# One unrolled pipeline over single batches in place of two looped stages at the end of a six-stage kernel

## The reference, cut to what matters

```python
# fifth block: x are the latents, ctx_1024 the context
xn, ln_lat = layer_norm(ctx, g1, b1), layer_norm(latents, g2, b2)
q = ln_lat @ Wq
kv = jnp.concatenate([xn, ln_lat], axis=1) @ Wkv
weight = jnp.einsum('bhld,bhnd->bhln', q * scale, k * scale)
weight = softmax(jnp.where(full_mask, weight, neg))
out = einsum('bhln,bhnd->bhld', weight, v) ... @ Wout
# sixth block
h = bitlinear(x, norm1_w, w1)        # rmsnorm, rows rounded to 8 bits, weights to -1, 0, 1
h = act_scale * jnp.square(jax.nn.relu(h)) + act_bias
y = bitlinear(h, norm2_w, w2)
```

## Time and profile before

| | us |
|---|---|
| median of 3 runs (lowest, highest) | 2016.25 (2013.10, 2018.52) |
| profiled execution, device time | 2015.99 |
| its span in the trace | 2014.2 |
| latents phase, first context load to barrier | 1183.9 to 1825.7 |
| last phase (its weights rounded by 1834.2) | 1828.6 to 2014.2 |
| DVE busy in the last 17.0 us of the latents' setup | 1.53 |

### The profile page before, as it was taken

How to read it: one execution, slowest core, us unless ns; L and a number is a source line. 1 busy time by engine, 2 the same in 40 slices (tenths; PEclk the granted TensorE clock), 3 DMA queues, 4 the chain that set the end, 5 groups by cost and what they waited for, 6 DMA issues and landing times. The chain is left out here.

```text
span 2014.2 us, 28424 instructions
## 1 busy us (share of the span) xinstructions
PE 1525.4 (76%) x10850; PEld 793.9 (39%) x10850; DVE 1358.7 (67%) x2359; ACT 829.6 (41%) x1141; POOL 361.7 (18%) x309
## 2 busy tenths in 40 slices
PE   5788767777778768888888738999999999983222
PEld 3555444454433323333333424444444444431111
DVE  3765655767555579888888617575675675466997
ACT  2222122322234358888888723332332332313444
POOL 2232212323200021111110013332322322120000
PEclk9889868887778879999999959999999999996555
DMA  3000000000000000000000010000000000000000
GB/s 135 1 1 2 1 11 12 6 12 6 1 0 0 0 1 1 1 1 1 1 1 1 1 53 6 6 5 0 5 5 0 5 0 0 0 0 0 11 10 21
DMA packets 14814, 16.46 MB, mean 8 GB/s; under 512 B 640, under 2 KB 13056, under 8 KB 14336
## 3 DMA queue, kind: packets, MB, share of 16 engines
q1 hardware_dynamic: 14432, 14.47, 2.1%
q10 hardware_dynamic: 288, 0.67, 0.1%
HBM read 13.04 MB, written 2.10 MB: 8 GB/s over the span
## 5 line engine op out<-in xcount | busy, mean ns | idle before, releaser
L1427 POOL PARTITION_BROADCAST l_share<-l_recip x128 | 103.9, 812 | 376.5 <-issue 207.0
L1283 ACT ACTIVATE l_prob<-psum,l_bias_now 128x1024 f32<-128x1024 f32 x64 | 71.3, 1114 | 221.3 <-PE psum L1191 221.3
L1349 DVE TENSOR_REDUCE l_top<-psum 128x8 bf16<-128x1024 f32 x64 | 77.3, 1207 | 126.2 <-PE psum L1177 124.5
L1216 PE MATMUL psum<-l_prob,l_X 128*128 128x512 f32 x256 | 124.9, 611 | 12.7 <-DVE l_px L1343 12.7
L1185 PE MATMUL psum<-l_th,l_XT 128*128 128x512 f32 x256 | 126.0, 615 | 7.2 <-ACT l_prob L1283 7.2
L1343 DVE TENSOR_TENSOR l_px<-psum,l_share 128x1024 f32<-128x1024 f32 x64 | 78.0, 1219 | 71.7 <-PE psum L1216 45.3
L1161 PE MATMUL psum<-l_XT,l_A 128*128 128x512 f32 x256 | 117.5, 604 | 9.3 <-ACT l_XT L1269 9.3
L1240 PE MATMUL psum<-l_px,l_N 128*128 128x512 f32 x256 | 111.5, 593 | 2.1 <-DVE l_px L1343 2.1
L1337 DVE CAST l_th<-l_th 128x512 bf16<-128x512 f32 x128 | 89.3, 739 | 29.2 <-ACT l_th L1272 29.2
L1356 DVE RECIPROCAL l_recip<-psum 128x512 f32<-128x512 f32 x32 | 107.1, 3347 | 0.7 <-PE psum L1206 0.6
L1272 ACT COPY l_th<-psum 128x512 f32<-128x512 f32 x128 | 74.2, 586 | 74.5 <-PE psum L1161 74.5
(11 more groups left out here) (301 smaller groups left out, 3309.2 us busy)
## 6 DMA issues: line engine op xcount, KB each, us to landing
early_weights<-in_weights SPq DMA_DIRECT2D x1, 2405.0 KB, 15.1
c_cs<-in_ctx SPq DMA_DIRECT2D x8, 256.0 KB, 2.8
l_mats<-in_l_mats SPq DMA_DIRECT2D x1, 2048.0 KB, 8.0
l_craw<-in_ctx SPq DMA_DIRECT2D x8, 256.0 KB, 2.8
out<-b_normed SPq DMA_DIRECT2D x8, 256.0 KB, 2.3
late_weights<-in_weights SPq DMA_DIRECT2D x1, 1089.0 KB, 11.0
relbias<-in_relbias ACTq DMA_DIRECT2D x1, 512.0 KB, 4.9
early_weights<-in_weights SPq DMA_DIRECT2D x1, 385.0 KB, 4.2
```

What stands on the lines that cost most here:

```text
L1216: last = nc.tensor.matmul(ps[:, 4 + q, :], X[:, b, :], prob[:, b % 4, q, :], start=True, stop=True)
L1349: nc.vector.tensor_reduce(top[:, b % 4, :], ps[:, 0:2, :].rearrange("p a (j n) -> p (a j) n", n=P), AX.X, ALU.max, negate=True).then_inc(s ...
L1427: nc.gpsimd.partition_broadcast(share[:, p % 2, n // 2, n % 2, :], recip[32 * n:32 * n + 1, p % 2, :], P).then_inc(s["share"], 1)
```

## The change

The two phases become `latents_bitlinear_phase`, unrolled over steps i from -9 to 89, one batch a step. Work that was done per group of 8 batches is now done per quad of 4 (two tiles): `job(i, first)` names the quad whose piece falls on step i, `chunk` a quad and one of four parts. PE's heads come in four chunks of four heads, 256 columns wide, and so does `combine`. The casts to bf16 move from DVE to POOL's tensor_copy, one per chunk (128x1024), the product with the second norm weight moves from DVE to POOL (`normed_hidden`, 128x1024), and the pieces of the quantised layer are set between the latents' steps on each engine. The weights are rounded in the setup. The barrier and the norm phase between the two phases are gone; the output is stored by 16 DMAs, context loads are 16 instead of 8. `spread`, `invert`, `divide`, `row_tops`, `scores`, `shift` keep their shapes. Sections left out of the diff below are helpers whose shapes follow from this.

```diff
-def latents_phase(nc, ctx, c, name):
...
+def latents_bitlinear_phase(nc, ctx, c, name, out):
...
+    QB = 4
+    Q = B // QB
+    TQ = 2
...
+    craw, lat, cx = sb("craw", [P, 2, TQ, P]), sb("lat", [P, TQ, P]), sb("cx", [P, TQ, P])
+    gx = sb("gx", [P, 2, TQ, P])
+    XT, XT16 = sb("XT", [P, 3, QB, 2, S]), sb("XT16", [P, 3, QB, 2, S], BF16)
+    X = sb("X", [P, 2, QB, P])
...
+    FIRST, LAST = -9, B + 26
+    RO, SC, GA, SU, YB = 0, 2, 4, 6, 7
+
+    def job(step, first):
+        n, rest = divmod(step - first, QB)
+        return n if rest == 0 and 0 <= n < Q else None
+
+    def chunk(step, first):
+        n, k = divmod(step - first, QB)
+        return (n, k) if 0 <= n < Q else (None, None)
...
+            def heads(q, k):
+                if QB * q + k >= 1:
+                    pe.wait_ge(s["th_sb"], QB * q + k)
+                pe.wait_ge(s["XT_sb"], q + 1)
+                for j in range(QB):
+                    last = nc.tensor.matmul(ps[:, RO + j // 2, (j % 2) * 256:(j % 2 + 1) * 256], A[:, QB * k + j, :], XT[:, q % 3, :, 1, :],
+                                            start=True, stop=True)
+                last.then_inc(s["th_ps"], 1)
+
...
+            def gather(b):
+                q, k = divmod(b, QB)
+                pe.wait_ge(s["X_sb"], q + 1)
+                pe.wait_ge(s["exped"], b + 1)
+                if b >= 1:
+                    pe.wait_ge(s["px_sb"], b)
+                for n in range(2):
+                    last = nc.tensor.matmul(ps[:, GA + n, :], X[:, q % 2, k, :], prob[:, b % 4, n, :], start=True, stop=True)
+                last.then_inc(s["px_ps"], 1)
...
+            for i in range(FIRST, LAST):
+                banks_free(i)
+                if 0 <= i < B:
+                    scores(i)
+                    shift(i)
+                q, k = chunk(i, -5)
+                if q is not None:
+                    heads(q, k)
+                if job(i, 13) is not None:
+                    pairs = min(max(0, (i - 2) // 2 + 1), B // 2)
+                    pe.wait_ge(s["recip"], pairs)
+                    tokens_turned(job(i, 13))
+                if 0 <= i - 2 < B:
+                    gather(i - 2)
+                if i % 2 == 1 and 0 <= i < B:
+                    if job(i, 13) is not None:
+                        pe.wait_ge(s["xiT_sb"], job(i, 13) + 1)
+                    if job(i - 1, 22) is not None:
+                        pe.wait_ge(s["d_read"], job(i - 1, 22) + 1)
+                    sums((i - 1) // 2)
+                if 0 <= i < B:
+                    pe.wait_ge(s["exped"], i + 1)
+                if job(i, -6) is not None:
+                    columns_in(job(i, -6))
+                if job(i, 0) is not None:
+                    keys_back(job(i, 0))
+                if job(i, 10) is not None:
+                    turn_back(job(i, 10))
+                if job(i, 15) is not None:
+                    hidden(job(i, 15))
+                if job(i, 21) is not None:
+                    hidden_turned(job(i, 21))
+                if job(i, 22) is not None:
+                    pe.wait_ge(s["recip"], min(i // 2, B // 2))
+                    if job(i - 1, 13) is not None or job(i - 9, 13) is not None:
+                        pe.wait_ge(s["xiT_sb"], min(Q, (i - 13) // QB + 1))
+                    down(job(i, 22))
+                q, k = chunk(i, 6)
+                if q is not None:
+                    combine(q, k)
+                if 0 <= i + 1 < B:
+                    q, k = chunk(i, -5)
+                    if q is not None:
+                        pe.wait_ge(s["th_sb"], QB * q + k + 1)
+                    rough(i + 1)
...
+            def roots_of(q1, q2, q3):
+                if q1 is not None:
+                    act.wait_ge(s["var1"], q1 + 1)
+                    nc.scalar.activation(roots[:, :, :], roots[:, :, :], ACT.Sqrt).then_inc(s["root1"], 1)
...
+            for i in range(FIRST, LAST):
+                if 0 <= i < B:
+                    exponent(i)
+                q, k = chunk(i, -5)
+                if q is not None:
+                    keep_heads(q, k)
+                if job(i, 13) is not None:
+                    tokens_turned(job(i, 13))
+                if i % QB == 3:
+                    roots_of(job(i, 11), job(i, 19), job(i, 23))
+                if job(i, -6) is not None:
+                    keep_columns(job(i, -6))
+                if job(i, 0) is not None:
+                    keep_keys(job(i, 0))
+                if job(i, 15) is not None:
+                    activate(job(i, 15))
+                if job(i, 21) is not None:
+                    hidden_turned(job(i, 21))
+                if job(i, 9) is not None:
+                    keep_y(job(i, 9))
+                if job(i, 18) is not None:
+                    measure(job(i, 18))
...
-            def heads(g, gathered, prepare_next):
-                head = Count(g, H)
-                for h in range(H):
-                    if h in BETWEEN and gathered is not None:
-                        divide(gathered, BETWEEN[h])
-                    if h == 4 and prepare_next:
-
-                        prepare(g + 1, Count(g, 1)(1))
-                    dve.wait_ge(s["th_sb"], head(h + 1))
...
+            def residual(q):
+                x = stream[:, TQ * q:TQ * q + TQ, :]
+                dve.wait_ge(s["yt_ps"], q + 1)
+                nc.vector.tensor_tensor(x, ps[:, SC, 0:256].rearrange("p (t d) -> p t d", d=P), x, ALU.add).then_inc(s["out_read"], 1)
+                dve.wait_ge(s["out_read"], q + 1)
+                for t in range(TQ):
+                    last = nc.vector.bn_stats(stats[:, t, :], stream[:, TQ * q + t, :])
+                step(last)
+                for t in range(TQ):
+                    last = nc.vector.bn_aggr(mom1[:, t, :], stats[:, t, :])
+                step(last)
+                step(nc.vector.tensor_scalar(roots[:, 0, :], mom1[:, :, 1], LN_EPS, None, ALU.add))
+                step(nc.vector.reciprocal(roots[:, 1, :], roots[:, 0, :]))
+                step(nc.vector.tensor_tensor(roots[:, 1, :], roots[:, 1, :], mom1[:, :, 1], ALU.mult))
+                nc.vector.tensor_scalar(roots[:, 1, :], roots[:, 1, :], EPS_NORM, None, ALU.add).then_inc(s["var1"], 1)
...
+            def quantise(values, to, scales, biggest, inverse):
+                step(nc.vector.tensor_tensor(biggest[:, :], biggest[:, :], inverse, ALU.mult))
+                step(nc.vector.tensor_scalar(biggest[:, :], biggest[:, :], EPS_Q, None, ALU.max))
+                step(nc.vector.reciprocal(scales[:, :], biggest[:, :]))
+                step(nc.vector.tensor_scalar(scales[:, :], scales[:, :], 127.0, None, ALU.mult))
+                step(nc.vector.tensor_tensor(scales[:, :], scales[:, :], inverse, ALU.mult))
+                for t in range(TQ):
+                    last = nc.vector.tensor_scalar(values[:, t, :], values[:, t, :], scales[:, t:t + 1], MAGIC, ALU.mult, ALU.add)
+                step(last)
+                return nc.vector.tensor_scalar(to[:, :, :], values[:, :, :], MAGIC, 127.0, ALU.subtract, ALU.min)
...
+            def tokens(q):
+                dve.wait_ge(s["root1"], q + 1)
+                step(nc.vector.reciprocal(roots[:, :, :], roots[:, :, :]))
+                for t in range(TQ):
+                    tile = TQ * q + t
+                    last = nc.vector.tensor_scalar(stream[:, tile, :], stream[:, tile, :], mom1[:, t, 0:1], roots[:, 0, t:t + 1],
+                                                   ALU.subtract, ALU.mult)
+                step(last)
+                step(nc.vector.tensor_tensor(xn[:, :, :], stream[:, TQ * q:TQ * q + TQ, :],
+                                             w("b_n1").unsqueeze(1).to_broadcast([P, TQ, P]), ALU.mult))
+                step(nc.vector.tensor_reduce(amax[:, :], xn[:, :, :], AX.X, ALU.max, apply_absolute_value=True))
+
+            def tokens_quantised(q):
+                if q >= 1:
+                    dve.wait_ge(s["x_ps"], q)
+                quantise(xn, xi, xscale, amax, roots[:, 1, :]).then_inc(s["x_ready"], 1)
+                if q >= 1:
+                    dve.wait_ge(s["r_sb"], TQ * q)
+                nc.vector.tensor_scalar(deq[:, :], amax[:, :], 1.0 / 127.0, wmean[:, 0:1], ALU.mult, ALU.mult).then_inc(s["deq1"], 1)
...
+            def scaled_hidden(q):
+                dve.wait_ge(s["squared"], q + 1)
+                if q >= 1:
+                    dve.wait_ge(s["hn"], q)
+                    dve.wait_ge(s["ss2"], q)
+                nc.vector.tensor_scalar(hh[:, :, :], r[:, :, :], w("b_as"), w("b_ab"), ALU.mult, ALU.add).then_inc(s["hh"], 1)
+
+            def hidden_biggest(q):
+                dve.wait_ge(s["hn"], q + 1)
+                step(nc.vector.tensor_reduce(amax2[:, :], hn[:, :, :], AX.X, ALU.max, apply_absolute_value=True))
+
+            def hidden_quantised(q):
+                dve.wait_ge(s["root2b"], q + 1)
+                step(nc.vector.reciprocal(ss2[:, :], ss2[:, :]))
```

(121 more changed lines are left out.)

679 lines of the change are left out of this document (245 added, 434 removed).

## The result

The changed kernel took **2122.37 us** (median; 2114.17 to 2124.49), the kernel before 2017.38 in the same comparison: ratio 1.0511, 95% interval 1.0473 to 1.0550. It is slower, by 105 us; 2168 was predicted, and 2055 to 2250 as the range. The profiled execution has a span of 2119.1 us.

What follows compares the result with a forecast made beforehand. PE bounds the latents' stage and DVE the last phase; the merged stage was to wait on POOL's switches. 35 + 5 x 50 + 9 x 59 + 2 x 49 + 68 = 982 us from 1183.9 gave 2168 us, range 2055 to 2250.

Steps and rivals of the forecast that it cites:

- case 4: The main forecast: every inverse in full quads waits 8.0 us for its shares; 2105 to 2225 us, chance 0.50.
- A: First step of a quad (i divisible by 4), with a spread and `prepare`'s products; 16.9 us in a full quad.
- full quads: Quads of steps 20 to 55, with POOL products between any two spreads; 59 us each, nine of them.
- C: Third step of a quad, with a spread and `normed_hidden`; shares at 41.6 us, step over at 47.5 in full quads.
- The way back: POOL's switch from broadcasts to the first tensor_tensor product after them; 7.1 us.
- the other two signs: Signs of error: `divide` waits 2 us throughout, or `row_tops` waits for PE rather than stands behind `divide`.
- lower bound of 52 us: Full quad if the copy costs 1.9, POOL is back in time, nothing queues at the port and the clock holds.
- B: Second step of a quad; maxima at 18.1 us after PE idles, 2.0 us lost to the clock; forecast 11.3.
- D: Fourth step of a quad, with gather, `divide`, `prepare` and `hidden_biggest`, 2.0 us lost to the clock; forecast 11.5.
- 1: Rival: no reconfiguration between product and broadcast in unrolled code, shares 2.2 us after every inverse; 1964 us, chance 0.10.
- Rival 2: The waits are paid but cheaper, with a cheap copy and the clock held; 2055 to 2105 us, chance 0.20.
- Rival 3: POOL becomes the bound, by dear copies or copies with their own reconfiguration; 2225 to 2330 us, chance 0.17.

Runs made afterwards that it cites:

- e2: The changed kernel with `normed_hidden` and `prepare`'s seven products moved from POOL to DVE; 1966.47 us, 0.9742 of the kernel before.
- e12: The kernel before with `prepare`'s seven products moved to DVE, so POOL does only broadcasts in the phase; 2020.00 us, 1.0014.
- e10: e2 with gather and `divide` three steps behind, `hidden_biggest` one step earlier, token rounding and `down_read` one later, all ahead of `divide`; 1894.68 us, 0.9389.
- e13: e10 with the 64 casts moved back from POOL to DVE, one at the end of each step; 1904.91 us, 0.9451 of the kernel before.
- e3: The changed kernel with `prepare`'s products two steps earlier, behind `normed_hidden`, all still on POOL; 2082.67 us, 1.0319 of the kernel before.
- e14: The changed kernel with an unread 128-element broadcast on POOL behind each `prepare` and each `normed_hidden`; 2036.04 us, 1.0087 of the kernel before.

## Why the prediction was right, and where its numbers were off

The mechanism is the predicted one, case 4: the switches, paid in the wait between the inverse and `divide`. The products on POOL explain the whole loss: the order gains 54 us (e2 against e12) and they cost 156 (2122 against 1966). Term by term, from the starts of the maxima (the first at 1212.36, those of each A, the last at 2032.49):

| term | predicted us | measured us |
|---|---|---|
| head | 35 | 30.2 |
| quads of steps 0 to 19 | 5 x 50 = 250 | 220.1 (34.8, 43.6, 43.7, 47.9, 50.1) |
| full quads | 9 x 59 = 531 | 514.4 (56.2 to 58.2, mean 57.2) |
| steps 56 to 59 | 49 | 49.1 |
| steps 60 to 63 and tail | 49 + 68 = 117 | 123.1 |
| sum | 982 | 936.9 |

- **Pairs**: 26 before the spreads and 26 before the products, as counted. Shares: inverse to `divide` 8.4 in A and 8.1 in C, 8.0 forecast; 204 us in all, "some 200". The way back took 7.0. The Trainium skill (GPSIMD Engine Reference, Instruction dispatch) has some 6 us for the first call of a freshly loaded function, after such a record; the 6.5 and 7.0 of this trace agree.
- **The cast** was a mis-sized term: 1.04 us, where I took 3.5 and put the lower bound at 1.9. "The copy is far from 3.5" was one of the three signs of being wrong, and it came true; the waits on the shares did not depend on it, and the other two signs did not appear. The nearest row, POOL's product with two inputs, bounds a copy with one input from above and not from below. The Trainium skill (GPSIMD Engine Reference, Elementwise — side-by-side cycle accounting) gives 2.6 cycles an element for a product with two inputs, 1.03 for the smallest loop bodies and some 1.8 at best for a tight unrolled loop. From the product's 2.35 us the last two are estimates of 0.93 and 1.63; the 1.04 of this trace lies near the first, and which of them stands for a copy no run here shows. What followed from it failed too: in a full quad POOL is not back late for C's inverse. It is through at 1632.69 when that inverse ends at 1637.20. That is 0.5 of the 1.4 us by which C is shorter than forecast (`divide` starts 8.1 us after the inverse, not 8.6); the pieces behind `divide` give another 0.6. So the copy's price hardly moved the full quads. The lower bound of 52 us needed a held clock and no queue at the port as well, and those two took 4.4 and 1.8 us. `normed_hidden` took 2.35 and not 1.9.
- **The early quads** carry 30 of the 45 us that the sum is too high, and 28 of those lie in the first three (122.1 us for 150). The step that failed is the list of DVE's pieces: `tokens` comes first at step 12 and `residual` at step 10, but I charged A with 2.1 us of `tokens_quantised` and 1.0 behind the copy, and C with 2.1 of `residual` and 1.0, from step 0 on. The starts of A's and B's maxima in the third and the fourth quad:

```profile
1290.78 1.23 DVE L1473 TENSOR_REDUCE l_top<-psum 128x8 bf16<-128x1024 f32 x1 [0.61 <-PE psum L1277]
1299.11 1.22 DVE L1473 TENSOR_REDUCE l_top<-psum 128x8 bf16<-128x1024 f32 x1 [0.50 <-PE psum L1277]
...
1334.46 1.23 DVE L1473 TENSOR_REDUCE l_top<-psum 128x8 bf16<-128x1024 f32 x1 [0.61 <-PE psum L1277]
1345.60 1.22 DVE L1473 TENSOR_REDUCE l_top<-psum 128x8 bf16<-128x1024 f32 x1
```

A takes 8.3 us without these pieces and 11.1 with them, as forecast. The very first quad has only one spread besides. The fourth and fifth quad took 98.0 us for 100; in them the cheap copy shortened C to 16.2 us from 20.2, because POOL is in time and `divide` starts 8.0 us after the inverse instead of 11.3, but B took 10.6 for 8.8.
- **Full quads**: A 17.1, B 12.2, C 17.9, D 10.8 in the quad shown, forecast 16.9, 11.3, 19.3 and 11.5. B's 0.9 us more is the clock's.
- **The clock**: 0.86 over the full quads. The heads took 3.73 us after B's idle stretch and 3.05 after D's, for 1.95 in A: 1.8 and 1.1. With the shift (1.04 and 1.03 for 0.62) and B's gather (2.59 for 1.88) it is 2.9 in B and 1.5 in D, forecast 2.0 each. In e2 and e10, without the stretches, it was 0.95 and 1.00.
- **DVE beside POOL**: the scaling of two values begun at 1618.40 lasts to 1619.38, the cast's end, 0.98 for its usual 0.17; with an earlier product of the chain (0.59 us for 0.16, beside the last broadcast) it is 1.2 in A, and 0.6 in C, where I had 1.0 each. The rule of the Trainium skill (SBUF — State Buffer, Who interferes with whom), that the later one is blocked for the other's whole instruction, agrees with this trace and with e10; it costs little because the copy is short.
- The Trainium skill's doubt about moving work from DVE to POOL (Perfetto Trace Analysis, Optimizing Scalar/DVE Operations) is half borne out: four fifths of the saving was lost to blocked operations, and e10 still leads e13 by 10 us.
- **The tail** was 6 us short with its quad, within its 15. That the rounding is hidden in the setup was not tested by itself. The 24 small DMAs of the prediction are 32 by the changes listed above it (16 loads and 16 stores); between 1212 us and the end only one wait on a DMA is in the trace, of 1.4 us, on the output.
- **Rivals**: 1 is out in the changed kernel (26 pairs), but its price, 1964 us, is what e2 measured with one pair, 1966. That is close partly by chance: e2's full quads take 44.6 us for 42.7, its five early ones 199.0 for 213.5. Rival 2 missed by 17 us; its cheap copy was right and its held clock was not. Rival 3 is out: it needed dear copies or copies with a reconfiguration of their own, and the copy took 1.04 us and has no record.

Open: why e3 waits longer for its gathers.

## What to carry to other kernels

Before a POOL queue is interleaved more finely, count how often it goes from elementwise products to partition_broadcast and back: each way cost 6 to 7 us here however small the operations, and is taken only when POOL comes to the instruction, so an idle POOL does not absorb it. Keep one kind of work on POOL (the most by far), or let the consumer come a step later, or issue a small broadcast early. Bound an unseen operation by rows that do more and rows that do less, not by two that both do more.

## What the runs showed of the hardware that was not expected

- The switch is set off by the next broadcast in POOL's queue, not by the wait ahead of it: a broadcast of 128 elements (0.43 us) placed early took all 28 pairs, and the spreads had none (e14). It helped only where POOL was idle between the products and the inverse: `divide` then waited 0.34 us in A, but 6.77 in C.
- A tensor_copy on POOL (128x1024, f32 to bf16) took 1.04 us, under half of a product of that size (2.35), and set off no switch, either before or behind broadcasts.
- A single-element product costs as much in switches as a 128x1024 one: 32 of them 203 us.
- DVE operations on 128x2 that began beside a POOL copy took up to 1.03 us for 0.16.
- The records alone are no price: e12 has 12 of them though POOL does only broadcasts there, with one wait on issue in 32 spreads.
